# Layer 0 by halves of the output columns, with the two parts of x side by side in products of 512 columns

## What is computed

```
x = x + (x @ W0.T + b0 + coeff[b] * (x @ (2*mask[b] - 1)))     # layer 0, mask is 8 x 1024 x 1024 int32
x = x + x @ w_eff.T          # layer 1, w_eff: quantised weight plus a product of rank 64
x = x + x @ W2 + b2 + 2 * (x @ A2[slot]) @ B2[slot]            # layer 2, rank 16 per batch
x = x + (x @ B3[slot].T) @ A3[slot].T                          # layer 3, rank 16 per batch
```

## Time and profile before

| | us |
|---|---|
| median of 3 runs | 572.14 (571.79 to 572.32) |
| profiled execution, its own time | 572.8 |
| its span in the trace | 571.0 |
| PE busy | 551.2 (97%) |
| DVE, ACT, POOL busy | 386.2, 307.9, 127.8 |
| granted clock of PE | full from first slice to last |

### The profile page before, as it was taken

How to read it: one execution, slowest core, us unless ns; L and a number is a source line. 1 busy time by engine, 2 the same in 40 slices (tenths; PEclk the granted TensorE clock), 3 DMA queues, 4 the chain that set the end, 5 groups by cost and what they waited for, 6 DMA issues and landing times.

```text
span 571.0 us, 9937 instructions
## 1 busy us (share of the span) xinstructions
PE 551.2 (97%) x3492; PEld 497.8 (87%) x3492; DVE 386.2 (68%) x583; ACT 307.9 (54%) x551; POOL 127.8 (22%) x134
## 2 busy tenths in 40 slices
PE   5889999999998899999999999999999999999997
PEld 4788888888887798998899899899889989989986
DVE  5999778988836894674766668467486666846521
ACT  3686756786635754454553555445455455544510
POOL 2679658987711001001000000100100000010000
PEclk9999999999999999999999999999999999999999
DMA  7865041843259791970781493097077149404201
GB/s 223 267 63 134 20 120 51 240 126 110 75 152 325 231 270 42 222 218 20 156 250 53 124 232 122 37 221 219 18 160 240 59 122 221 135 37 149 74 20 55
DMA packets 125898, 80.10 MB, mean 140 GB/s; under 512 B 91504, under 2 KB 107888, under 8 KB 125872
## 3 DMA queue, kind: packets, MB, share of 16 engines
q1 hardware_dynamic: 125296, 78.71, 49.4%
q0 software_dynamic: 288, 1.05, 0.5%
q10 hardware_dynamic: 288, 0.01, 0.0%
HBM read 65.59 MB, written 14.16 MB: 140 GB/s over the span
## 4 chain that ended last, share of the span: by engine, by line
PE 87%; DVE 6%; DMA 3%; ACT 2%; SPq 1%; issue 1%; DVEq 0%; ACTq 0%
PE bank L1339 10%; PE bank L1340 10%; PE bank L1341 10%; PE bank L1319 10%; PE bank L1321 10%; PE bank L1320 10%; PE bank L1208 6%; PE bank L1210 6%; PE bank L1209 6%; PE bank L1114 2%; DMA mask_ring<-in_mask_Bx4096x_ik 2%; PE bank L1348 1%; PE bank L1347 1%; PE bank L1355 1%; PE bank L1132 1%; DMA codebook_rows<-in_condB_codebook 1%
## 5 line engine op out<-in xcount | busy, mean ns | idle before, releaser
L1319 PE MATMUL bank<-x_t_hi,m_hi 128*128 128x256 f32 x512 | 145.3, 284 | 5.1 <-DVE m_lo L1015 2.7
L1320 PE MATMUL bank<-x_t_lo,m_hi 128*128 128x256 f32 x512 | 144.9, 283 | 0.0
L1321 PE MATMUL bank<-x_t_hi,m_lo 128*128 128x256 f32 x512 | 144.9, 283 | 0.0
L700 ACT CAST m_hi<-merged_ring 128x512 fp32r<-128x512 f32 x128 | 77.0, 618 | 83.8 <-PE bank L1321 56.1
L1015 DVE TENSOR_TENSOR m_lo<-merged_ring,m_hi 128x512 fp32r<-128x512 f32 x128 | 84.5, 690 | 32.5 <-ACT m_hi L700 32.5
L1319 PEld LDWEIGHTS bank<-x_t_hi,m_hi 128*128 128x128 f32 x512 | 98.2, 192 | 6.4 <-DVE m_lo L1015 6.1
L1339 PE MATMUL bank<-P_hi,x_t_hi 128*128 128x512 f32 x256 | 99.8, 390 | 0.0
L1340 PE MATMUL bank<-P_lo,x_t_hi 128*128 128x512 f32 x256 | 99.8, 390 | 0.0
L1341 PE MATMUL bank<-P_hi,x_t_lo 128*128 128x512 f32 x256 | 99.6, 389 | 0.0
L1320 PEld LDWEIGHTS bank<-x_t_lo,m_hi 128*128 128x128 f32 x512 | 98.2, 192 | 0.3
L1321 PEld LDWEIGHTS bank<-x_t_hi,m_lo 128*128 128x128 f32 x512 | 98.2, 192 | 0.0
(11 more groups left out here) (147 smaller groups left out, 895.3 us busy)
## 6 DMA issues: line engine op xcount, KB each, us to landing
mask_ring<-in_mask_Bx4096x_ik SPq DMA_DIRECT2D x64, 512.0 KB, 4.0
x_squares<-in_x SPq DMA_DIRECT2D x64, 128.0 KB, 3.0
out<-out_staged SPq DMA_DIRECT2D x32, 256.0 KB, 2.0
w_nat<-in_L_cond_W SPq DMA_DIRECT2D x15, 512.0 KB, 4.9
w_raw<-in_L_cond_weight SPq DMA_DIRECT2D x16, 256.0 KB
g_batch<-g_dram SPq DMA_DIRECT2D x32, 128.0 KB, 3.9
w0t_dram<-w_out SPq DMA_DIRECT2D x14, 256.0 KB, 2.2
w_t<-w0t_dram SPq DMA_DIRECT2D x7, 512.0 KB, 8.7
```

The source lines that it names most:

```text
L700: nc.scalar.copy(Mh[:, n % MR], ring_f[:, k % MR, h * HALF:(h + 1) * HALF]).then_inc(s["h_set"], 1)
L1319: mm(dst, mh, xTh[:, k], start=(k == 0 and o % 2 == 0), stop=False, skip_group_check=True)
L1320: mm(dst, mh, xTl[:, k], start=False, stop=False, skip_group_check=True)
L1321: ins = mm(dst, ml, xTh[:, k], start=False, stop=(k == KT - 1), skip_group_check=True)
```

## The change

Three edits are made at once.

1. Layer 0. `xTh` and `xTl` become the two halves of one tile `xThl`, and PE multiplies M_hi by both in one matmul of 512 columns, whose bank then holds hi*hi in its columns 0 to 255 and hi*lo in 256 to 511; M_lo by `xTh` is added to the first half as before. An output block fills a whole bank, so the eight blocks use all eight banks, and `main` and `rank` share them (`L0_BANK`, `MAIN_BANK`, `RANK_BANK`). Tile n is now 8h + k: first all k of output half 0, then those of half 1. A mask part holds two row blocks by half the columns. x1 is made from two halves of a bank: ACT copies one with the bias (`x1_part`), DVE adds the other (`x1_sum`), ACT rounds (`x1_hi`), then GpSimd (first four blocks) or DVE (last four) makes the rest. The first four are done beside half 1 of layer 0. `rank` has eight matmuls of 512 in place of 16 of 256.
2. Batch 0. x of batch 0 has a place of its own and is loaded some 20 us of program order earlier, GpSimd makes its lo part; masks and W0's transpose are loaded in another order and by other waits.
3. `bb`. The column of b2 becomes column 129 of `b2t`, so one matmul of 129 columns stands for each pair; ACT copies the column.

The diff, cut to its core:

```diff
-    xTh = at("x_t_hi", [P, KT, T], F32R, reg_z1 + 48 * KB)
-    xTl = at("x_t_lo", [P, KT, T], F32R, reg_z1 + 56 * KB)
-    x1h = at("x1_t_hi", [P, KT, T], F32R, reg_z1 + 64 * KB)
-    x1l = at("x1_t_lo", [P, KT, T], F32R, reg_z1 + 72 * KB)
+    xThl = at("x_t_pair", [P, KT, 2, T], F32R, reg_z1 + 48 * KB)
+    xTh, xTl = xThl[:, :, 0, :], xThl[:, :, 1, :]
+    x1hl = at("x1_t_pair", [P, KT, 2, T], F32R, reg_z1 + 64 * KB)
+    x1h, x1l = x1hl[:, :, 0, :], x1hl[:, :, 1, :]
+    x1s = at("x1_sum", [P, KT, 2, T], F32, reg_z1 + 64 * KB)[:, :, 1, :]
...
+        L0_BANK = [3, 6, 7, 0, 4, 5, 1, 2]
+        MAIN_BANK = [3, 6, 7, 4]
+        RANK_BANK = 5
...
+            def load_w0t(j):
+                ks = part_rows(j) if j % HT < HT - 1 else slice(KT - 2, KT - 1)
+                last = ks.stop - 1
+                sp.wait_ge(w0_out_stored[j // HT], 16 * (last + 1))
+                sp.wait_ge(s["p_used"], KT * (G - 1) + (4 * last + 16) // 5)
+                sp.dma_start(w0t[:, ks, part_cols(j)], w0t_dram[ks, :, part_cols(j)].rearrange("k p n -> p k n")).then_inc(w0t_in[j], 16)
...
-            sp.wait_ge(s["normed"], HT * 2 * G)
-            load_x(0, range(1))
+            sp.wait_ge(s["delta_done"], 2 * G)
+            load_x(0)
+            (blk, _h0), _h1 = w0_halves(G - 2)
+            store_w0t(blk, 0)
+            load_w0n(G - 1)
+            sp.wait_ge(s["pool_added"], 2 * G)
+            load_mask(0, 1)
             sp.wait_ge(s["eff_set"], 2 * G)
             load_mask(0, 0)
-            load_mask(0, 1)
-            sp.wait_ge(s["p_used"], KT * (G - 1))
-            load_x(0, range(1, 2))
+            store_w0t(blk, 1)
             for h in range(2):
                 sp.wait_ge(w0_out_stored[h], 16 * (G - 1))
-            for k in range(2):
-                load_w0t(k)
             load_mask(0, 2)
             sp.wait_ge(s["w0_tr"], 2 * G)
             load_mask(0, 3)
-            for k in range(2, KT - 1):
-                load_w0t(k)
+            for j in range(KT):
...
+            for i in range(4):
+                pool.wait_ge(s["xt_hi"], i + 1)
+                ks, toks = slice(i // 2 * HT, (i // 2 + 1) * HT), slice(i % 2 * P, (i % 2 + 1) * P)
+                nc.gpsimd.tensor_tensor(xTl[:, ks, toks], xs0[:, i % 2, ks, :], xTh[:, ks, toks].bitcast(F32), ALU.subtract).then_inc(s["xt_first"], 1)
...
+            with pool.Fori(0, NB - 1) as b:
+                x1_lo(b)
+                pool.wait_ge(s["u_done"], b + 1)
+                c_copies(b + 1)
+            x1_lo(NB - 1)
...
-            act.wait_ge(s["p_used"], KT * (G - 1) + 5)
+            act.wait_ge(s["p_used"], KT * (G - 1) + 4)
             x_hi(0, range(2))
             m_hi(0, 0, True)
-            p_hi(G - 1)
-            signs(0, 2)
+            p_hi(G - 1, range(1))
+            x_hi(0, range(2, 4))
             m_hi(0, 1, True)
-            signs(0, 3)
+            for k in range(2, MR):
+                signs(0, k)
+            p_hi(G - 1, range(1, 3))
+            for h in range(2):
+                w0_evac(G - 1, h)
...
+                nc.scalar.activation(x1s[:, o], bank[L0_BANK[o]][:, T:2 * T], ACT.Identity, bias=b0c[:, o:o + 1]).then_inc(s["x1_part"], 1)
...
+                nc.scalar.copy(x1h[:, o], x1s[:, o]).then_inc(s["x1_hi"], 1)
...
+                    if k == MR + 1:
+                        for o in range(HT):
+                            x1_part(b, o)
+                    if k == MR + 2:
+                        for o in range(HT):
+                            x1_hi(b, o)
...
-            dve.wait_ge(s["p_used"], KT * (G - 1) + 5)
-            x_lo(0, range(2))
+            dve.wait_ge(s["p_used"], KT * (G - 1) + 2)
             m_lo(0, 0)
-            p_lo(G - 1)
             merged(0, 1, True)
+            p_lo(G - 1, range(1))
...
+                nc.vector.tensor_tensor(x1s[:, o], x1s[:, o], bank[L0_BANK[o]][:, 0:T], ALU.add).then_inc(s["x1_sum"], 1)
...
+            def batch(b, first=False, last=False, second=False):
                 if not first:
-                    for k in range(2):
-                        merged(b, k, first)
+                    merged(b, 0, first)
+                    out_add(b - 1, 0, 1, second)
+                    merged(b, 1, first)
                     for k in range(2):
                         m_lo(b, k)
-                for k in range(2, 3 if first else MR + 2):
-                    merged(b, k, first)
-                if not first:
-                    out_add(b - 1, 1)
+                    merged(b, 2, first)
+                    merged(b, 3, first)
+                    out_add(b - 1, 1, 0)
+                    merged(b, MR, first)
+                    out_add(b - 1, 1, 1)
+                    merged(b, MR + 1, first)
+                else:
+                    merged(b, 2, first)
+                    p_lo(G - 1, range(1, 3))
                 for k in range(2, KT):
                     if first and k + 1 < KT:
                         merged(b, k + 1, first)
                     m_lo(b, k)
-                    if first and k == 3:
-                        x_lo(0, range(2, 4))
                     if not first and k >= MR and k + 2 < KT:
                         merged(b, k + 2, first)
+                    if k == MR + 1:
+                        for o in range(HT):
+                            x1_sum(b, o)
...
-                    mm(bank[MISC][:, 0:NBR], b3t[:, k], b2t[:, k], start=(k == 0), stop=(k == KT - 1), skip_group_check=True)
-                    ins = mm(bank[MISC][:, NBR:NBR + 1], b3t[:, k], b2c[:, k:k + 1], start=False, stop=(k == KT - 1), skip_group_check=True)
+                    ins = mm(bank[MISC][:, 0:NBR + 1], b3t[:, k], b2t[:, k], start=(k == 0), stop=(k == KT - 1), skip_group_check=True)
...
-                        mm(dst, mh, xTh[:, k], start=(k == 0 and o % 2 == 0), stop=False, skip_group_check=True)
-                        mm(dst, mh, xTl[:, k], start=False, stop=False, skip_group_check=True)
-                        ins = mm(dst, ml, xTh[:, k], start=False, stop=(k == KT - 1), skip_group_check=True)
...
+                for h in range(2):
+                    for k in range(KT):
+                        n = KT * h + k
+                        pe.wait_ge(s["m_ready"], 2 * KT * b + n + 1)
+                        if first and h == 0 and k % HT == 0:
+                            pe.wait_ge(s["xt_first"], 2 * (k // HT) + 2)
+                        if not first and n == 0:
+                            pe.wait_ge(s["xt_ready"], 4 * b)
+                        for j in range(HT):
+                            o = HT * h + j
+                            if k == 0:
+                                layer0_bank_free(b, o, first)
+                            full = bank[L0_BANK[o]][:, :]
+                            cols = slice(j * P, (j + 1) * P)
+                            mh, ml = Mh[:, n % MR, cols], Ml[:, n % MR, cols]
+                            mm(full, mh, xThl[:, k].rearrange("p i t -> p (i t)"), start=(k == 0), stop=False, skip_group_check=True)
+                            ins = mm(full[:, 0:T], ml, xTh[:, k], start=False, stop=(k == KT - 1), skip_group_check=True)
+                            if j == HT - 1:
+                                ins.then_inc(s["m_used"], 1)
+                            elif k == KT - 1:
+                                ins.then_inc(s["l0_done"], 1)
...
+                    ins = mm(bank[RANK_BANK][:, :], ck, x1hl[:, k].rearrange("p j t -> p (j t)"), start=(k == 0), stop=(k == KT - 1))
...
-                main(b, 0, 0, range(KT), first)
-                main(b, 0, 1, range(0, 1), first)
-                if first:
-                    pe.wait_ge(s["terms"], 5 * 2 * G)
-                else:
-                    pe.wait_ge(s["u_ready"], b)
+                main(b, 0, 0, range(HT))
+                main(b, 0, 1, range(HT))
                 rank(b)
-                main(b, 0, 1, range(1, 5), first)
+                main(b, 0, 0, range(HT, KT))
+                main(b, 0, 1, range(HT, KT))
                 close(b, 0, 0)
-                main(b, 0, 1, range(5, KT), first)
                 close(b, 0, 1)
                 for h in range(2):
-                    main(b, 1, h, range(KT), first)
+                    main(b, 1, h, range(KT))
                     close(b, 1, h)
```

More of the change, by code:

```diff
@@ L1329, in main @@
+            def main(b, t, h, ks):
+                o = bank[MAIN_BANK[2 * t + h]][:, :]
                 toks = slice(t * P, (t + 1) * P)
@@ L1331, in main @@
                 for k in ks:
[L1332 to L1338 removed]
+                    if t == 0 and h == 0 and k < HT:
+                        pe.wait_ge(s["x1_ready0"], HT * b + k + 1)
                     mm(o, x1h[:, k, toks], Ph[:, k, cols], start=(k == 0), stop=False)
```

214 lines of the change are left out of this document (112 added, 102 removed).

## The result

The changed kernel takes 578.94 us (median of 4 runs, 578.82 to 580.39) against 572.23 us in the same session: 1.0114 of the kernel before, 95% interval 1.0085 to 1.0144. It is slower by 6.7 us, where 7.7 us faster was forecast, and it lies outside the range. (Every ratio here compares undisturbed runs with undisturbed runs, so it can differ a little from the ratio of two medians.) The profiled execution spans 576.7 us; the one before spanned 571.0.

The account below looks back on a forecast made before the run. The prediction took PE, busy 97% of the span, to bound the kernel. It summed 572.8 - 5.97 - 0.53 - 1.78 - 0.2 + 0.7 = 565.0 us profiled, so 564.4 as median, with a range of 560.5 to 569.5.

Parts of the forecast that it names:

- The half turn: Batches 1 to 7, new x1 work behind tile 11; 0.7 us lost in all. H is tile 8's start on PE.
- tile 12: Batches 1 to 7: 0.2 us of slack, 0.1 lost each; batch 0: 1.5 us lost to last mask and x1 work.
- The pair: Layer 0: one wide and one narrow product take 0.3483 us against 0.3600 for three narrow ones, 5.97 us less.
- Rival 2: Layer 0: the product of 512 gets no cheaper, a pair takes 0.36 as before; median 570.8 us; chance 0.10.
- Batch 0: Layer 0's start and gaps in batch 0: 5.5 us lost against 5.7 before, 0.2 less. E is group 7's end.
- output block 3: Batch 0: its bank must first be left by P_lo, which ends at E + 2.3; 1.2 us lost.
- tile 4: Batch 0: ACT has other work ahead of its m_hi, so it comes at E + 8.4; 1.6 us lost.
- tile 6: Batch 0: needs the fifth mask part, behind six loads of W0's transpose; ready at E + 12.4, 1.2 us lost.
- The start of layer 0: Batch 0: PE starts at once after group 7; the 2.6 us wait before the first product is gone.
- `rank`: Each batch: 16 matmuls at 1.92 us become 8 at 1.85, 0.07 a batch, 0.53 us less in all.
- `bb`: Ahead of group 7's end: eight pairs of products become eight single ones, 1.78 us less; bounds 0 and 2.0.
- Rival 1: Half turn: GpSimd beside DVE holds DVE up, tile 14 costs 1.2 us a batch; median 573.2 us; chance 0.09.

Follow-up runs that it names:

- x_late: The changed kernel with the loads of the next x (batches 2 to 7) issued after masks 6 and 7 instead of ahead of them; 570.08 us.
- final: Changed kernel, signs of mask 7 behind tile 13's m_hi, next x issued after masks 6 and 7, batch 0's mask 4 ahead of the last two w_t loads; 565.06 us.
- final_grouped: The kernel `final`, but with the four products of 512 columns of a tile ahead of its four of 256; 564.12 us.
- x1_on_dve: The changed kernel with the four x1_lo of the first half on VectorE, after the last m_lo, instead of on GpSimd; 579.03 us.

## Why the prediction was wrong

In the profiled execution the forecast was a span of 571.0 - 7.8 = 563.2 us; it was 576.7. The 13.5 us between, step by step:
- **The half turn, 7.6 us, is the step that failed.** The text put the signs of mask 7 at H + 0.7 and summed ACT and DVE from there, to 0.2 us of slack at tile 12; that the mask has landed by then was taken over from the kernel before without a row. The mask held the signs until H + 2.8 in batch 1 (H = 246.5), and until H + 1.6 to H + 3.4 in batches 2 to 6. The sum of engine times was sound, even cautious: with the signs at H + 0.7, as in `x_late`, there was no gap, and by the 1.17 us found above some 0.4 us of slack, not 0.2. Over 22.60, layer 0 of batches 1 to 6 lost 8.3 us instead of 0.7. The prediction did write that nothing in the trace shows 2 KB pieces, and then looked for their price in batch 0 alone.
- **The pair, 2.5 us, is a term mis-sized.** 0.353 instead of 0.3483: layer 0 is 64 pairs in 22.60. Over eight batches 3.5 us were won, not 5.97, below the lower end of 4.2. From start to start, meaned over batches 1 to 7 of `final`, the narrow product takes 0.117, as forecast, and the wide one 0.236, more than in the mixture of the earlier trace rows (0.2317). Grouped, as in `final_grouped`, they take 0.1185 and 0.232; in `main` the wide one still takes 0.227. Why a wide product costs more in layer 0 stays open. Rival 2 (0.36) did not come.
- **Batch 0, 4.0 us.** PE started at once, then lost 1.0 at output block 3 (forecast 1.2), 2.1 at tile 4 (1.6), 1.2 at tile 6 (1.2) and 2.5 at tile 12 (1.5): 1.3 us more than the 5.5 written. Mask 4's signs were set at E + 9.3 = 187.3 and came at 189.3: the mask is issued behind all eight w_t loads, not six; that tile 6 lost no more than forecast is because PE came to it late, at half clock. The fall of the clock was in no step, 3.4. Against that, the kernel before lost 6.4 in this batch, where I had added up 5.7: 2.62 ahead of it, and 26.79 - 23.03 = 3.76 in it.
- The start of layer 0 was 0.2 us earlier than forecast, and `rank` gave 0.13 a batch instead of 0.07, 0.4 more. `bb` was right in its place, at 1.84, and alone worth 3.0 in time.

These add up to 7.6 + 2.5 + 4.0 - 0.6 = 13.5.

Rival 1 named a time near the measured one (573.2, up to 577 with tile 12 held) and a gap of the right size, by luck: its mechanism is wrong, as `x1_on_dve` and `x_late` show from both sides. It priced tile 14, and the gap was at tile 12, whose m_lo was not slowed. The mark that the prediction set for it, a gap at tile 12 or a slow m_lo, could not tell it from a late mask; the row that could is ACT's wait for the DMA.

`final` takes 565.06 us, near the forecast of 564.4, but that is no proof of the sum. It has three edits more, and in its span of 562.9 us the pairs still won 2.5 us less than forecast, while batch 0 (1.3), the half turn (0.7), the start (0.5) and `rank` (0.4) came out better and made up for it.
